# Key and query projections of the first attention layer: two half steps against one whole step

## What is computed

```python
def _L0_xattn_ref(x, mask, kv, kv_mask, Wq, bq, Wk, bk, Wv, bv):
    bs, c, t1 = x.shape              # 8, 256, 512
    h = 16; d = c // h; scale = 1.0 / math.sqrt(d)
    q = jnp.einsum('oc,bct->bot', Wq, x) + bq[None, :, None]
    k = jnp.einsum('oc,bct->bot', Wk, kv) + bk[None, :, None]
    v = jnp.einsum('oc,bct->bot', Wv, kv) + bv[None, :, None]
    ...                              # 16 heads of 16 channels, 512 positions
    attn = softmax(where(kv_mask, (q * scale) @ k, -inf))
    mean = attn @ v
    ex2 = attn @ (v * v)
    std = jnp.sqrt(jax.nn.relu(ex2 - mean * mean))
    return (_masked_instance_norm(x, mask) * std + mean) * mask
```

## Time and profile before

| | |
|---|---|
| median of three runs | 1879.78 us |
| profiled execution, time of the run | 1875.84 us |
| profiled execution, span | 1874.0 us |
| TensorE busy over the span | 1739.7 us (93%) |
| VectorE busy | 1369.2 us (73%) |
| ScalarE busy | 1080.4 us (58%) |
| GpSimd busy | 343.0 us (18%) |

### The profile page before, as it was taken

One profiled execution on the slowest core, in us unless ns is written; L12 is line 12 of the kernel. 1 busy time (PEld: TensorE's weight loads), 2 busy tenths in 40 slices (PEclk: granted clock), 3 DMA queues, 4 the chain that ended last, 5 costly groups with the idle time before them and its releaser, 6 DMA issues. The chain is left out here.

```text
span 1874.0 us, 34298 instructions
## 1 busy us (share of the span) xinstructions
PE 1739.7 (93%) x12328; PEld 1198.4 (64%) x12328; DVE 1369.2 (73%) x2843; ACT 1080.4 (58%) x2419; POOL 343.0 (18%) x392
## 2 busy tenths in 40 slices
PE   5999999999999988899989988999999599999998
PEld 2344343333334334778778877788888489999997
DVE  4778887888889864899898988899999653333332
ACT  1565666666666654777777777777777551111111
POOL 0001121122112122133222312233332040000000
PEclk7899999999999989899999999999999799999999
DMA  3011010101100022223223434333333050000000
GB/s 106 9 36 50 13 50 13 48 26 37 49 14 27 15 92 63 83 69 81 67 67 99 102 92 108 86 86 94 94 92 96 29 157 12 11 11 11 11 13 21
DMA packets 75688, 105.03 MB, mean 56 GB/s; under 512 B 21392, under 2 KB 36240, under 8 KB 75280
## 3 DMA queue, kind: packets, MB, share of 16 engines
q1 hardware_dynamic: 65040, 82.08, 15.9%
q0 software_dynamic: 8192, 16.79, 3.7%
q10 hardware_dynamic: 2304, 4.20, 0.8%
HBM read 39.55 MB, written 4.72 MB: 24 GB/s over the span
## 5 line engine op out<-in xcount | busy, mean ns | idle before, releaser
L477 DVE TENSOR_REDUCE nmax<-ps 128x2 f32<-128x1024 f32 x256 | 311.2, 1220 | 118.9 <-PE ps L355 117.9
L658 ACT ACTIVATE prob<-ps 128x1024 f32<-128x1024 f32 x256 | 261.8, 1023 | 214.0 <-PE ps L367 213.4
L1404 ACT ACTIVATE at_prob<-at_t,at_nmax 128x256 f32<-128x256 f32 x512 | 256.6, 505 | 106.7 <-DVE at_nmax L1207 98.6
L382 PE MATMUL ps<-prob,v 128*64 128x512 f32 x1024 | 284.6, 635 | 0.0
L1207 DVE CUSTOM_DVE_ANT_0 at_t<-at_t,at_off 128x256 f32<-128x256 f32 x512 | 236.5, 498 | 8.9
L1726 ACT ACTIVATE mlp_h<-ps,b 128x256 f32<-128x256 f32 x128 | 53.8, 472 | 270.0 <-PE ps L1661 270.0
L1765 DVE CAST mlp_h_hi<-mlp_h 128x512 fp32r<-128x512 f32 x64 | 29.3, 458 | 220.8 <-ACT mlp_h L1726 220.8
L1562 POOL TENSOR_TENSOR at_low<-at_low,at_high 128x512 fp32r<-128x512 f32 x64 | 85.7, 1339 | 498.2 <-DVE at_high L1233 498.2
L1038 PE MATMUL ps<-ident,at_prob 128*128 128x128 f32 x1024 | 160.4, 280 | 1.4 <-ACT at_prob L1404 1.4
L1027 PE MATMUL ps<-at_k_stack,at_q_stack 96*128 96x256 f32 x512 | 119.0, 315 | 36.6 <-ACT at_prob L1404 30.8
L1661 PE MATMUL ps<-mlp_x_hi,mlp_w_hi 128*128 128x256 f32 x512 | 145.9, 285 | 6.6 <-DVE mlp_w_lo L1750 6.5
(11 more groups left out here) (203 smaller groups left out, 4320.5 us busy)
## 6 DMA issues: line engine op xcount, KB each, us to landing
at_k_stack<-at_high SPq DMA_DIRECT2D x256, 64.0 KB, 2.4
at_q_stack<-at_high SPq DMA_DIRECT2D x128, 64.0 KB, 2.7
at_q_stack<-at_high POOLq DMA_DIRECT2D x128, 64.0 KB, 2.4
at_q_stack<-at_low SPq DMA_DIRECT2D x128, 64.0 KB, 2.1
at_k_stack<-at_low POOLq DMA_DIRECT2D x128, 64.0 KB, 2.3
mlp_w_in<-in_w SPq DMA_DIRECT2D x32, 256.0 KB, 3.1
c_in<-in_ctx SPq DMA_DIRECT2D x8, 512.0 KB, 4.3
X<-in_x SPq DMA_DIRECT2D x8, 512.0 KB, 5.0
```

The lines of the kernel that those rows point to most:

```text
L382: mm = eng.matmul(ps[2 * QD * k:2 * QD * (k + 1), VB, :], v[:, c, HG * G + 2 * p + k, :], prob[:, M % PROBS, k, :], start=(c == 0), stop=( ...
L477: eng.tensor_reduce(nmax[:, n % 2, j, 2 * p:2 * p + 2], ps[:, at:at + 2, :], AX, ALU.max, negate=True).then_inc(s_max, 1)
L658: eng.activation(prob[:, M % PROBS, :, :], ps[:, ST:ST + 2, :], ACT.Exp).then_inc(s_exp, 1)
L1404: ins = eng.activation(prob[:, m % 2, i, :], t[:, p, i, :], ACT.Exp, scale=-1.0, bias=nmax[:, m % 4, i:i + 1], accum_out=z[:, T % 2, j, 2 ...
```

## The change

`items_at` put the first half of the query projection into step 0 and the second into step 1, and the halves of the key projection into steps 3 and 4. Now both halves of the query stand in step 1 and both of the key in step 4. The order of the items, their number and what they wait for are the same; part 0 is issued a step later.

```diff
@@ def items_at(w, s):
-        if s in (0, 1, 3, 4) and w + 1 < GROUPS:
-            return [("k" if s > 2 else "q", w + 1, (s % 3,))]
+        if s in (1, 4) and w + 1 < GROUPS:
+            return [("k" if s > 2 else "q", w + 1, (0, 1))]
         if s == 2 and 0 <= w - 1 < GROUPS:
             return [("turn", w - 1, (0, 1))]
```

## The result

The changed kernel takes 1891.48 us in the median (1880.24 to 1896.97, nine runs) against 1879.78 (1866.88 to 1886.21, nine runs, the three of the table among them) of the kernel before: ratio 1.0072, interval 1.0045 to 1.0100. It is slower, by less than 1%, and 1.5 us over the predicted 1890. A second trace of the same kernel, further down, shows more of it.

A forecast was written before the change was run, and what follows sets the result against it. First layer: TensorE's pace, with empty steps bound by a TensorE-ScalarE loop that a projection half hides. 8.0 - 0.3 + 0.6 + 2.1 = 10.4 us on 1879.78 gave 1890, range 1880 to 1900.

The forecast's parts named there:

- Query side: Steps 0 and 1: 2.57 + 2.57 = 5.14 us become 1.88 and 3.25, together 5.13; taken as 0 for 31 groups.
- rival A: Saved visits count: emptied steps take 1.68 us each, 62 x 0.2 = 12.6 us less, 1867; chance 0.08.
- Key side: Steps 3 and 4: step 3 gains 0.15 us, step 4 grows by 0.684, net +0.53 us per group.
- Item 1: Odd groups w = 3 to 29 and w = 4: 15 x 0.53 = 8.0 us, less 0.3 for w = 7.
- Item 2: Group w = 2, still on batch 0's plain products: 0.6 us more, bounds 0.5 and 0.9.
- Item 3: Root groups w = 8, 12, 16, 20, 24, 28: longer step 4 fits into 1.58 us idle before step 5's turned scores; 0.
- Item 5: Group w = 30: ScalarE waits for GpSimd's product before its square, and TensorE for both; 0.
- Item 4: Groups w = 6, 10, 14, 18, 22, 26, with GpSimd's product: 6 x 0.35 = 2.1 us, bounds 0 and 0.53 each.
- Item 6: Groups w = 0 and 1: later query start wins about 0.6 us, delayed scores lose about 0.5; together 0, bounds -1 and +1.
- Rival B: Delay hidden because VectorE or GpSimd's DMA chain sets most groups' length: 0 to 5 us, 1880 to 1885; chance 0.15.
- rival D: TensorE's stand in step 3 drops its clock: ten steps at 0.9 us, +9 on top of 10.4, 1899; chance 0.15.
- The signs named beforehand: Query steps 1.88 and 3.25, key steps 2.42 and 3.25; wrong if full item under 0.90 + 0.684 or VectorE's maxima end waits.

The follow-up runs named there:

- the key alone: Kernel before with only the key halves merged, both in step 4, query halves left in steps 0 and 1: 1892.16 against 1878.07 us, ratio 1.0074.
- the kernel with the late second query: Changed kernel with ScalarE's second query moved from step 2 to step 4: 1864.47 us, ratio 0.9927 to the kernel before; measured again, 1866.51, ratio 0.9943.

## Why the prediction was right, point by point

- **Direction, size and mechanism: right.** 1890 predicted, 1891.48 measured. The step that carried the sum, ScalarE's backlog losing its cover in step 3, is shown by the waits (8 to 36), by the key alone (1.0074), and by both cures: the key one step earlier (steady groups 601.27 us instead of 613.03), or the second query out of the backlog (601.46, and 0.9927 in all). That the total came within 1.5 us is partly luck, as the last point shows.
- **Query side, 1.88 and 3.25: right** in nearly all groups. That the saved visit (0.216) is given back to the exponential held, so **rival A fell**. (Its 62 x 0.2 is 12.4, not 12.6.) Of the rule that changing TensorE's tiling mode drains it (the Trainium skill, TensorEngine Tiling (Array Packing), Key Properties), the price agrees with the rows, 3.25 being 2.57 plus 0.68 and not plus 0.90; in the pair of steps the gain is used up by the empty step's 1.88.
- **Key side, +0.53 per group: mis-sized, +0.63.** The failed term is "they start at 556.58 and no earlier", which took the empty step's 0.05 between an exponential's end and its scores. Behind the exponential that follows the turned copy it was 0.14 to 0.15, here and in the kernel with the late second query; why it is longer there isn't shown. Step 3 won 0.05 rather than 0.15.
- **Item 1, odd groups at 0.53: mis-sized.** Groups 3, 4 and 5 lost 0.61 to 0.63, but 9 to 29 only 0.31 to 0.38. I had written that nothing later in these groups absorbs the delay. The value projection did: before, it waited for VectorE's raw key in a step of 3.90, now VectorE, which is delayed by less than TensorE, is through in time and the step is 3.66. Counted by the groups: 15 x 0.53 became about 1.9 + 3.9 for 14 of them. **Item 2, w = 2 at 0.6: right** (0.63).
- **Item 3, roots at 0: right, by more than its reason.** The idle time before the exponential was there, but what holds the end of these groups is VectorE's low key in step 7, which the prediction doesn't have. Three of six are 0.00 or -0.01, and at w = 24 the turned scores start at 538.86 in both traces, behind a wait of 0.95 now and 1.58 before: 0.63 shorter, where some 0.7 was named. The 1.33 and -0.88 of two others, and w = 7 (-1.7), come with steps lengthened in only one of the two traces. In the second trace of the changed kernel the six sum to +2.9: behind the wait for the low key, 1.97 us where it had mostly been 0.6 to 0.8, value products at the lower clock follow at w = 8, 20 and 24. **Item 5, w = 30 at 0: right** within a microsecond (-0.7, and +0.9 in the second trace).
- **Item 4, batch ends at 2.1: the step that failed.** 7.9 us in one trace and 11.5 in the other. Where nothing else happens the delay passes in full (0.66, not 0.35), 4.0 for six; the rest is nearly all the two collisions. I bounded a group by the delay, though I wrote that a later VectorE sometimes meets GpSimd at a worse place. That was no reason to lean to the upper bound, it was a bound of its own: 2.48 - 0.74 = 1.7 us for one more operation behind GpSimd, and some 1.5 for a fall of the clock behind the longer wait. Nor did I see that a query half covers GpSimd's delay in step 0 as a key half covers ScalarE's in step 3.
- **Item 6, the start at 0 with bounds of 1: failed.** It won 9.7 us in the trace and 11.7 in the second. I costed the matmuls at the clock of the kernel before, and never asked if a whole item at 22.93 would let the clock rise some 30 us sooner.
- **Rival B fell** (the delay isn't hidden), and **rival D** fell as it was put: the clock never fell behind the 0.35 us of step 3, where step 4 is 3.25 to 3.27 in every group but w = 2 and the roots groups. It fell behind waits of 1.85 us at batch ends and of 1.97 for the low key, but no longer behind the roots groups' waits for the exponential: 2 places against 6 before in the first trace, at a granted clock of 0.99 against 0.97, and 7 in the second.
- **The signs named beforehand.** The steps came as named but for step 3. The full item's 1.57 is 0.014 under the bound given for being wrong, which changes nothing in the sum, and the waits for VectorE's maxima grew from 9.5 to 10.8 us, while those for the low key grew from 2.4 to 12.3: VectorE ends more of the waits than the prediction allowed.
- **The errors cancel.** From the forecast's +10.4 to the trace's +4.4: items 1 and 2 about -2 without w = 7, item 4 +5.8, the start -9.7, w = 7 and 30 -2.4, later layers +2.1, the roots +0.2. The total came out better than its working deserves. The medians' +11.7 can't be split like this; the second trace has -11.7 at the start and +20.1 in the steady groups.

## What to carry to other kernels

Work between two waits is cover: before moving it, ask which backlog of which engine it hides, and whether that engine is late there; the same item made its pair of steps 0.63 us longer in step 4 and not at all in step 3. If it must be moved, move the other engine's optional work too: here an operation that could wait two steps took a loss of 0.7% away, and what the change gained at the start was left, 0.6 to 0.7%. And a delay of half a microsecond is not bounded by half a microsecond where it changes which of VectorE's operations meets one of GpSimd's.

## What the runs showed of the hardware

- The exponential behind ScalarE's turned copy let TensorE go 0.14 to 0.15 us behind its recorded end (27 times in the changed kernel's first trace); one after an idle gap, 0.05 to 0.06 (78 times). No gap is not the whole reason: twelve exponentials that started without one behind another operation, such as a split of operands (L699), also showed 0.05 to 0.06.
- VectorE's two-input operations took 2.48 (L465, 0.74 where GpSimd had no product running) and 2.84 (L434, 0.68 elsewhere) where GpSimd's product of two tensors had started first, and VectorE's next work began only then.
- The granted clock of 20 to 60 us went with how the first query's matmuls came, in one block of 3.78 us or in two of 2.08: 0.66 to 0.91 against 0.50 to 0.57 over all 13 traces. A value projection of 3.78 us in the same stretch was followed by the lower level.
- In the six groups with roots, waits of 0.94 to 1.16 us for the exponential were not once followed by value products at the lower clock before the wait for the low key (54 groups in nine traces); waits of 1.58 to 1.96 us were in 17 of 24 groups of the other four.
